# Wide cross attention computed with the queries on the partitions, probabilities transposed on TensorE

## What is computed

```python
q = (x @ Wq).reshape(b, n, heads, -1)
k = (ctx @ Wk).reshape(b, j, heads, -1)
v = (ctx @ Wv).reshape(b, j, heads, -1)
scale = q.shape[-1] ** (-0.5)
sim = jnp.einsum('bihd,bjhd->bhij', q, k) * scale
attn = jax.nn.softmax(sim, axis=-1)
out = jnp.einsum('bhij,bjhd->bihd', attn, v).reshape(b, n, -1)
return out @ Wo + bo
```

## Time and profile before

| | us |
|---|---|
| median of three runs | 5026.16 |
| profiled execution, its own time | 5027.45 |
| span of its trace | 5025.3 |
| busy: PE / PE weight load / DVE | 4277.7 / 2532.2 / 3372.2 |
| busy: ACT / POOL | 1921.6 / 1265.9 |
| mean granted TensorE clock, share of 2.4 GHz | 0.913 |
| wide cross stage of L2, from the trace | 2833 to 3336 |
| wide cross stage of L3, from the trace | 4416 to 4872 |

### The profile page before, as it was taken

The page is one execution under the profiler, slowest core; times in us unless marked ns, Lnnn a source line. Parts: engine busy times, 40 slices in busy tenths (PEclk is TensorE's granted clock), DMA queues, the critical chain, the costliest instruction groups (busy, mean ns, idle before and its releaser), DMA issues.

```text
span 5025.3 us, 55353 instructions
## 1 busy us (share of the span) xinstructions
PE 4277.7 (85%) x20572; PEld 2532.2 (50%) x20572; DVE 3372.2 (67%) x4878; ACT 1921.6 (38%) x2796; POOL 1265.9 (25%) x600
## 2 busy tenths in 40 slices
PE   6899989799988878888889667777999999967769
PEld 4343357434346745545555344456655555434448
DVE  4888765788866556676667565655677677746665
ACT  2556634355654523343334221223444444412111
POOL 1000011110001235545555411110444344500010
PEclk8999989899989979999999877788999999978879
DMA  3222230222223122222222232312222223143310
GB/s 114 40 39 45 44 67 16 51 52 39 36 42 62 37 59 59 59 60 59 59 58 54 62 73 64 67 46 60 63 59 65 61 60 78 38 93 74 73 42 19
DMA packets 157340, 282.21 MB, mean 56 GB/s; under 512 B 38234, under 2 KB 70292, under 8 KB 155920
## 3 DMA queue, kind: packets, MB, share of 16 engines
q1 hardware_dynamic: 157072, 278.67, 26.6%
HBM read 101.01 MB, written 25.23 MB: 25 GB/s over the span
## 4 chain that ended last, share of the span: by engine, by line
PE 60%; DVE 17%; issue 7%; ACT 5%; SPq 4%; POOL 4%; DMA 3%; DVEq 0%; POOLq 0%; ACTq 0%
PE PS L937 23%; PE PS L1093 11%; PE PS L1136 5%; PE PS L1013 4%; DVE PS L1698 4%; PE PS L1009 3%; DVE t L1621 3%; PE PS L1224 3%; PE PS L1107 2%; PE PS L1146 2%; SPq L2029 2%; POOL t L1876 2%; SPq L2042 2%; PE PS L1048 2%; DMA t<-t 1%
## 5 line engine op out<-in xcount | busy, mean ns | idle before, releaser
L937 PE MATMUL PS<-t 128*128 128x512 f32 (+7 forms) x7128 | 1942.7, 401 | 233.0 <-ACT t L1361 100.5
L1361 ACT ACTIVATE t<-PS 128x512 f32<-128x512 f32 (+3 forms) x1728 | 1238.9, 737 | 1503.5 <-PE PS L937 1497.0
L937 PEld LDWEIGHTS PS<-t 128*128 128x128 f32 (+4 forms) x7128 | 1160.8, 185 | 755.3 <-issue 217.2
L1093 PE MATMUL PS<-t 128*32 128x512 f32 (+3 forms) x4608 | 896.2, 618 | 0.2
L1617 DVE TENSOR_REDUCE t<-PS 128x1 fp32r<-128x1024 f32 x512 | 621.9, 1220 | 307.6 <-PE PS L1009 301.7
L1621 DVE TENSOR_REDUCE t<-PS 128x1 f32<-128x512 f32 x1024 | 649.1, 683 | 71.7 <-PE PS L1013 70.3
L1896 POOL TENSOR_TENSOR t<-t 128x1024 f32<-128x1024 f32 x256 | 620.8, 2425 | 146.9 <-ACT t L1361 122.1
L1698 DVE RECIPROCAL PS<-PS 128x256 f32<-128x256 f32 x256 | 449.5, 1756 | 12.5 <-PE PS L1107 12.5
L1840 POOL TENSOR_TENSOR t<-t 128x2048 f32<-128x2048 f32 x24 | 110.1, 4588 | 1237.7 <-DVE t L1508 631.9
L1013 PE MATMUL PS<-t 96*128 96x512 bf16 x1024 | 374.3, 395 | 37.5 <-DVE t L1621 14.1
L1009 PE MATMUL PS<-t 128*128 128x512 f32 x1024 | 341.1, 416 | 62.2 <-DMA t<-t 27.8
(11 more groups left out here) (127 smaller groups left out, 3763.5 us busy)
## 6 DMA issues: line engine op xcount, KB each, us to landing
t<-t SPq DMA_DIRECT2D x512, 128.0 KB, 3.5
t<-t SPq DMA_DIRECT2D x256, 256.0 KB, 3.9
t<-scr_n SPq DMA_DIRECT2D x288, 128.0 KB, 6.3
scr_n<-t SPq DMA_DIRECT2D x72, 256.0 KB, 2.2
t<-t SPq DMA_DIRECT2D x256, 64.0 KB, 2.0
t<-in_L_Wg SPq DMA_DIRECT2D x16, 768.0 KB, 4.6
t<-in_L_W SPq DMA_DIRECT2D x36, 256.0 KB, 3.2
t<-in_L_Wo SPq DMA_DIRECT2D x64, 128.0 KB, 2.6
```

The costliest lines, as they stand in the source:

```text
L937: ins = e.matmul(out, l, r, start=i == 0, stop=i == len(terms) - 1, tile_position=tp)
L1093: ins = e.matmul(banks[S.ot][wd * j:wd * j + wd, :], u.v[j][kt], P[0:S.pr, j, :], start=kt == 0, stop=kt == S.nkt - 1, tile_position=(0, w ...
L1361: e.activation(dst, src, ACT.Exp, scale=S.L.scale).then_inc(*expd.inc((S.i, i)))
```

## The change

In the two wide cross stages the scores are computed once, with 128 queries on the partitions and the keys as columns (step `cs`, one per unit and head). DVE reduces their negated maxima into `NM`; ACT takes the exponential with the maximum as a bias, one instruction for each tile of 128 queries, and accumulates the row sums into `SU`. DVE takes the reciprocal of 8 columns of sums, POOL multiplies the probabilities `PQ` by them (`cnorm`), TensorE transposes the eight 128 x 77 tiles (`cturn`), ACT copies them to `PT`, and `cav` multiplies by the values. `cmax`, `mturn`, its casts and DMAs, `score`, `sum` and the two `norm` steps are gone from these stages. The factor of 0.125 moves into the keys. The PSUM ring has three double banks (2-3, 4-5, 6-7), and `cav` uses banks 0 and 1 in turn. The keys are stored without gaps, 154 columns a head, and the 256 columns that a matmul reads run into the next head. Query projections, their weights, query stacks and the norms of the second batch stand half a unit to one unit earlier.

The diff, cut to its core (the steps `cs`, `cturn` and `cav` of TensorE, then `cs` and `cturn` of ScalarE, `cs` and `cnorm` of VectorE, `cnorm` of GpSimd):

```diff
+        if L.style == 64 and cross:
+            S.PQ = [sbt(c, [128, 2, 4, CT]) for _ in range(3)]
+            S.PT = [sbt(c, [CT, 2, 512]) for _ in range(2)]
+            S.NM, S.SU, S.RC = [[sbt(c, [128, 8]) for _ in range(3)] for _ in range(3)]
...
-            K.KXA, K.KXB_ = sbt(c, [128, 16, 256], F32R), sbt(c, [128, 16, 2 * CT], F32R)
+            K.keys = [sbt(c, [128, 16 * NW + 102], F32R) for _ in range(2)]
+            K.KXA, K.KXB_ = [k[:, 0:16 * NW].rearrange("p (h n) -> p h n", h=16) for k in K.keys]
...
+                    u.st = [[[(qs[:, j, 0, q0 + 128 * t:q0 + 128 * t + 128], K.keys[0][:, NW * h:NW * h + 256]),
+                              (qs[0:lim[j], j, 1, q0 + 128 * t:q0 + 128 * t + 128],
+                               K.keys[1][0:lim[j], NW * h:NW * h + 256])]
+                             for t in range(4)] for j, h in enumerate(u.heads)]
...
-                if S.cross:
-                    for at, step in ((1.5, ("av", S, n, 0)), (1.51, ("sum", S, n)), (1.52, ("fin", S, n)),
-                                     (1.9, ("norm", S, n, 0)), (2.2, ("norm", S, n, 1)), (2.9, ("proj", S, n, 0))):
-                        plan.put(n + at, 0, [step])
+        for u in S.units if S.cross else []:
+            for at, step in ((-1, ("cs", S, u.n, 0)), (-0.6, ("cs", S, u.n, 1)), (-0.3, ("cnorm", S, u.n)),
+                             (0.15, ("cturn", S, u.n)), (0.65, ("cav", S, u.n)), (0.66, ("fin", S, u.n)),
+                             (1.35, ("proj", S, u.n, 0))):
+                plan.put(u.n + at, 0, [step])
...
                     for g in range(2, 8):
-                        o, pg = 4 * g - 8, S.parts[g // 4]
+                        o, pg = 4 * g - 9, S.parts[g // 4]
                         plan.put(o, o, [("w_load", pg, g % 4)])
                         plan.put(o + 1.0, o + 1.0, [("w_split", pg, g % 4, int(g != 4))])
                         plan.put(o + 2.3, o + 3.7, nat64_steps(S, g, 0))
                     for pi in range(2, 16):
-                        plan.put(2 * (pi - 2), 2 * (pi - 2), [("qstack", S, pi)])
-                        plan.put(2 * pi - 3, 2 * pi - 1, max_steps(S, pi))
-                    plan.put(7.7, 10.1, norm_steps(nxt))
+                        plan.put(2 * pi - 4.5, 0, [("qstack", S, pi)])
+                    plan.put(6.75, 9.2, norm_steps(nxt))
...
+    wider = Ring([2, 4, 6], 1024)
...
+            elif what == "cs":
+                o, k, nth = take(w, ring, ("cs", S.i, n, j))
+                for t in range(4):
+                    ins = acc(o[:, 256 * t:256 * t + 256], u.st[j][t])
+                ins.then_inc(*bank_full[k].inc(nth))
+            elif what == "cturn":
+                w.wait_ge(p_normed, (S.i, n))
+                o, k, nth = take(w, ring, ("cturn", S.i, n))
+                for j in range(2):
+                    for t in range(4):
+                        ins = e.transpose(o[0:CT, 512 * j + 128 * t:512 * j + 128 * t + 128], S.PQ[n % 3][:, j, t, :],
+                                          ident[:, :])
+                ins.then_inc(*bank_full[k].inc(nth))
+            elif what == "cav":
+                for j in range(2):
+                    ins = e.matmul(banks[n % 2][64 * j:64 * j + 64, :], u.v[j], S.PT[n % 2][:, j, :], start=True, stop=True,
+                                   tile_position=(0, 64 * j))
...
+            elif what == "cs":
+                w.wait_ge(maxed, (S.i, n, j))
+                for t in range(4):
+                    at = slice(4 * j + t, 4 * j + t + 1)
+                    ins = e.activation(S.PQ[n % 3][:, j, t, :], o[:, 256 * t + CT * b:256 * t + CT * b + CT], ACT.Exp,
+                                       bias=S.NM[n % 3][:, at], accum_out=S.SU[n % 3][:, at])
+            elif what == "cturn":
+                e.activation(S.PT[n % 2][:, :, :], o[0:CT, :].rearrange("p (j q) -> p j q", j=2), ACT.Copy
+                             ).then_inc(*bank_free[k].nth(nth))
...
+            elif what == "cs":
+                v = o.rearrange("p (t c) -> p t c", t=4)[:, :, CT * b:CT * b + CT]
+                e.tensor_reduce(S.NM[n % 3][:, 4 * j:4 * j + 4], v, AX.X, ALU.max, negate=True
+                                ).then_inc(*maxed.inc((S.i, n, j)))
+            elif what == "cnorm":
+                e.reciprocal(S.RC[n % 3][:, :], S.SU[n % 3][:, :]).then_inc(*recip_made.inc((S.i, n)))
...
+            elif what == "cnorm":
+                w.wait_ge(recip_made, (S.i, n))
+                p = S.PQ[n % 3][:, :, :, :].rearrange("p j t k -> p (j t) k")
+                r = S.RC[n % 3][:, :].rearrange("p (i o) -> p i o", o=1).broadcast_to([128, 8, CT])
+                e.tensor_tensor(p, p, r, ALU.mult).then_inc(*p_normed.inc((S.i, n)))
```

More of the change, by code:

```diff
@@ L341, in attention_tiles @@
                 S.KS = [sbt(c, [128, 2, 2, N], F32R) for _ in range(2)]
-            if L.style == 64:
+            if L.style == 64 and not cross:
                 S.P = [sbt(c, [128, S.nh, 512]) for _ in range(S.npb)]
@@ L581, in max_steps @@
         if S.L.style == 64:
-            if S.cross:
-                out = [("cmax", S, m, j, q0) for j in range(2) for q0 in range(0, 8, 4)]
-            else:
-                out = [("max", S, m, j, qt, 0) for j in range(2) for qt in range(4)]
+            out = [("max", S, m, j, qt, 0) for j in range(2) for qt in range(4)]
             return out + [("mturn", S, m)]
@@ L594, in core64_steps @@
         k = S.nkt
-        for u in S.units:
+        for u in S.units if S.cross else []:
[3 more added lines that the diff above has]
+                plan.put(u.n + at, 0, [step])
+        for u in [] if S.cross else S.units:
             n = u.n
@@ L1019, in tensor_program @@
                 kv_ready(w, S)
-                if S.L.style == 64:
-                    o, k, nth = take(w, ring, ("max", S.i, m, j, q0))
-                    for i in range(4):
-                        ins = e.matmul(o[:, 256 * i:256 * i + 256], u.smq[j][q0 + i], u.smk[j], start=True, stop=True)
-                    ins.then_inc(*bank_full[k].inc(nth))
-                    continue
                 o, k, nth = take(w, ring, ("max", S.i, m, j, q0))
@@ L1033, in tensor_program @@
                     for j in range(2):
-                        k, nth = where["max", S.i, m, j, 4 if S.cross else 3]
+                        k, nth = where["max", S.i, m, j, 3]
                         w.wait_ge(bank_free[k], nth)
@@ L1040, in tensor_program @@
                 for q0 in range(0, S.nqt, 4):
-                    o, k, nth = take(w, ring if S.cross else small, ("turn", S.i, m, q0))
+                    o, k, nth = take(w, small, ("turn", S.i, m, q0))
                     o = o.bitcast(BF16) if S.L.style == 16 else o
@@ L1130, in tensor_program @@
                 if S.L.style == 64:
-                    k, nth = where["sum", S.i, n]
-                    w.wait_ge(bank_free[k], nth)
+                    if S.cross:
+                        w.wait_ge(o_out, (S.i, n))
+                    else:
+                        k, nth = where["sum", S.i, n]
+                        w.wait_ge(bank_free[k], nth)
                     w.wait_ge(wo_in[u.pi % 2], (S.i, u.pi))
@@ L1230, in tensor_program @@
                 else:
-                    ring = wide if then and then.L.style == 64 and then.kind != "kv" else attn
+                    ring = (wider if then.kind == "cross" else wide) if then and then.L.style == 64 else attn
                 small = one if ring is wide else ring
@@ L1339, in scalar_program @@
                 slot, was = p_slot(S, n, kt)
-                if S.cross and S.L.style == 64:
-                    w.wait_ge(zeroed, S.i)
                 if was and pr == 0:
@@ L2032, in sync_program @@
                     if old >= 0:
-                        w.wait_ge(scored, (S.i, 4 * old + 3 if S.cross else 16 * old + 15))
+                        if S.cross:
+                            k, nth = where["cs", S.i, 2 * old + 1, 1]
+                            w.wait_ge(bank_full[k], nth)
+                        else:
+                            w.wait_ge(scored, (S.i, 16 * old + 15))
                     q = slice(0, N) if S.cross else slice(512 * (n % 2), 512 * (n % 2) + 512)
@@ L2139, in _build @@
     uses[:] = [0] * 8
-    attn.n = updn.n = wide.n = one.n = 0
+    attn.n = updn.n = wide.n = one.n = wider.n = 0
     with nc.Block() as block:
```

108 lines of the change are left out of this document (62 added, 46 removed).

## The result

The changed kernel takes 4779.5 us in the median (4774.1 to 4782.0), the kernel before 5033.6 beside it (5020.5 to 5052.4): ratio 0.9491, interval 0.9456 to 0.9526. The forecast was 4907 with a range from 4790 to 5000. The profiled execution took 4777.2 us, 4775.4 of it span.

The account below looks back on a forecast made before the run. The bound was taken as a loop: sum matmul, reciprocals and multiplications, projection, add. New units of 11.3 us (L3) and 12.2 (L2) gave -57 and -62, so 5027.45 - 120 = 4907 us, range 4790 to 5000.

Parts of the forecast that it names:

- What bounds the kernel before, the loop through the reciprocals: Wide cross stages: sum matmul, two reciprocals and multiplications, projection and add form a loop of 10.5 us a unit.
- The loop of 8.3 us: New cross-stage unit at full clock: 4.3 us off TensorE from second scores to transposes, 4.0 on TensorE.
- The extras, 0.7 + 1.2 us a unit: Added to the loop: 0.73 for query matmuls; 1.2 for half of DVE's remaining work, the add and the norms' share.
- The clock, 0.85: TensorE's granted clock in the cross stages, 70% of the time at full, making 10.2 us a unit 11.3.
- L2's rotations, +0.9: L2's stage: POOL's rotary turn ahead of its multiply adds 3.6 us a group, 0.9 a unit, making 12.2.
- Stacks earlier, at nothing: Query stacks issued half a unit earlier on SP, some 40 us ahead of their first reader, costed at nothing.
- All banks freed before their turn: PSUM in the cross stages: all three double banks free in time; the scores' bank is held longest, about 2.3 us.
- PE loses 3.56 and gains 3.11, no gain: TensorE's work per cross-stage unit, in us: old matmuls and transposes dropped against new ones, no gain to speak of.
- More is hidden: Rival: accumulator free (loop 7.9), half the extras, clock 0.9; 9.98 us a unit in L3, 10.5 in L2; 4814; chance 0.24.
- The clock sinks: Rival: doubled transposes in bursts leave 40% of time at full clock; 12.7 and 13.6 us a unit; 4993; chance 0.12.
- The order eats it: Rival: work ahead in each queue counts in full, 3 us instead of 1.2, clock 0.8; time unchanged, 5027; chance 0.08.
- the slow exponential: Rival: ACT's exponential with accumulated sum is dear, deciding from 1.1 us each; at 1.3 the time is 5100; chance 0.08.

Follow-up runs that it names:

- e2: Kernel before with the reciprocals of the cross attentions left out, outputs multiplied by the sums instead; 4873.8 us, ratio 0.9676.
- e5: Changed kernel plus one unread VectorE maximum (about 1.2 us) per unit, right behind the addition of the projection's result; 4869.7 us.
- e6: Changed kernel plus the same unread VectorE maximum as e5, but right behind each unit's reciprocal; 4783.6 us.
- e7: Changed kernel with GpSimd's multiply of each unit done twice, the first time into a tile nobody reads; 4906.7 us.
- e3: Changed kernel with the multiply of probabilities by reciprocals moved from GpSimd to VectorE, behind its reciprocal; 4755.3 us.
- e11: Changed kernel with each score matmul of the cross attentions done twice into the same place; 4812.0 us.
- e1: Changed kernel with each unit's transposes, weighting and projection put half a unit later in TensorE's list; 4712.7 us, ratio 0.9353.
- e4: Changed kernel with two double banks of PSUM in the cross attentions instead of three; 4820.2 us.
- e8: Changed kernel with weight load, query stacking and first part of the next norm put back at their old plan positions; 4789.8 us.
- e9: e1 with the multiply of the probabilities moved to VectorE; 4735.8 us, ratio 0.9411.
- e12: Changed kernel with each unit's projection moved behind the weighting of the next unit in TensorE's order; 4726.5 us.

## Why the prediction was right or wrong

The mechanism was right: a loop that waits for POOL's multiply ahead of the transposes. What failed is the length of a unit at full clock, put at 8.3 + 0.7 + 1.2 = 10.2 us where the runs give some 8.5. By that figure 0.74 of the 1.7 us lie in the loop (7.56 in place of 8.3) and the larger part, some 1.0, in the extras: 0.9 in place of 1.9. The rest of the error, 0.5 of the 2.1 us in a period, is the clock.

- **What bounds the kernel before, the loop through the reciprocals:** right. e2 gives 160 us without them.
- **The loop of 8.3 us:** right in its parts and their order, 0.74 us too long. Off TensorE 3.76 in place of 4.3: the multiply took 1.22 (1.49 from rows without a broadcast operand), the four exponentials 1.33 (1.67), the handovers 0.54 (0.45). The accumulator was costed in the middle, 0.09 each; its read overlaps the next exponential, so the lower end was right. On TensorE 3.80 in place of 4.0.
- **The extras, 0.7 + 1.2 us a unit:** the step that failed most. Queries: 28.3/31 = 0.9 at the granted clock, about right (0.73 at full). Everything else came to 25.3/31 = 0.8 us with all dips of the clock in it, where I had 1.2 at full clock and the clock's share on top. "Half of DVE's 1.5 us" named no place on the loop; e5 and e6 show that such work costs 1.4 us a unit or nothing, by its place. Which of DVE's remaining instructions stand on the loop was not tested one by one.
- **The clock, 0.85:** it was 0.91 between L3's first and last transposes. In the working's own form, with 82% of the time at the upper of the two levels (2.4 GHz against 1.2), 1/(0.82/T + 0.18/15.1) = 9.23 gives T = 8.5 where I had 10.2. With the forecast's 10.2 and this clock the same form gives 10.8. So 1.6 of the 2.1 us were in the length of the unit and 0.5 in the clock. These are not independent: between L3's first and last transposes TensorE stood 2.4 us a unit in e7 and e5, 1.5 in the changed kernel, 1.2 in e3, 0.7 in e11 and 0.6 in e1, at clocks of 0.81, 0.85, 0.91, 0.94, 0.97 and 0.97. So a loop that is overestimated went with a clock that is underestimated, in the same direction. Two runs don't fit this row, e4 (0.90 at 2.1 us) and e2 (0.82 at 1.7), so the length of the wait alone doesn't make the clock.
- **L2's rotations, +0.9:** 1.15, right. **First transposes and tail:** right within 2 us. **Stacks earlier, at nothing:** e8 shows no difference. **All banks freed before their turn:** so in L3; in L2 `proj` waited 11.6 us for one. **PE loses 3.56 and gains 3.11, no gain:** its busy time fell by 62 and 59 us over the stages, to 281 and 266 where I had said about 310; by that working 14 of it is work, and I put the rest down to the clock.
- **Rivals.** *More is hidden* (4814, 9.98 and 10.5 us) is what came, and a little more; it had 0.24. Its ends for the accumulator and the extras were near the right ones, but the loop under it was still 7.9 where 7.56 came. *The clock sinks:* it rose. The rule of the Trainium skill (TensorE: Matmul & The Clock Gate, Part 4: PE-mode transpose), that transposes don't count as activity for the clock gate, would have made the doubled transposes pull it down; other matmuls surround them in every unit, so the runs bear out neither the rule nor its contrary, only that its consequence stayed away. *The order eats it* and *the slow exponential:* no sign of either; 0.30 us between exponentials, not 1.1.
- **The range** ended at 4790, at "more is hidden" with a clock of 0.95. All terms at their low ends together were never summed, and they err together: a shorter wait went with a higher clock in e1, e3 and e11.

## What to carry to other kernels

Write the loop out as a chain through each engine's order, and ask of each instruction whether it lies on it: one that does cost its whole length here, and one in the gap nothing (e5, e6), so never a share by halves. Where TensorE waits on such a loop, a microsecond more of it cost 1.2 to 1.6 (e5, e7), with a lower clock. When the loop is found, move it apart first: half a unit of lag in the plan gave 67 us here, after which moving work between engines (e3's 24 us) was worth less than nothing (e9). Then look at what binds next: it was a copy in ScalarE's queue in e12, and banks in L2 of e1.

## What was not expected of the hardware

- The exponential with an accumulated sum is two instructions of 324 and 203 ns, yet four of them in a row take 1.33 us: the second overlaps the next exponential.
- A multiply on GpSimd of 616 columns with a broadcast operand took 1222 ns, less than one of 512 columns without. VectorE took 800 ns for it.
- VectorE's cast of 512 columns takes 0.42 us, and 1.32 us beside that multiply (timeline of the changed kernel, L3):

```profile
4473.26 1.22 POOL L1939 TENSOR_TENSOR t<-t 128x616 f32<-128x616 f32 x1 [7.75 <-DVE t L1725]
4473.44 1.32 DVE L1572 CAST t<-t 128x512 fp32r<-128x512 f32 x1
```

  It ends 0.28 us after the multiply does. By the Trainium skill (SBUF — State Buffer, SBUF: two separate sides) GpSimd and VectorE share a pair of ports, and whichever instruction that needs the pair starts first holds it to its end, while the other waits. The trace agrees in kind: the multiply had started 0.18 us before the cast. Only 0.28 us of the cast lie behind the multiply, where it takes 0.42 alone; no run here explains the difference. It cost nothing in this unit, for VectorE still stood idle for 1.91 us ahead of its next add (L1769).
- With (238 - 219)/31 = 0.6 us a unit in which TensorE stood, the granted clock of a whole stretch full of transposes was 0.97 (e1); in the kernel before it was 0.79 with half as many.
